# A graph layer on one core: both count steps of a round in one PSUM tile, copied by one ScalarE instruction

## The chip, the core and the metric

The kernel runs on one core of a Trainium2 chip. The metric is the device time of one execution in microseconds (us), the median of several runs. Times inside one execution come from the hardware profiler.

## The reference

The layer has 6250 nodes with 64 features and 206250 edges, sorted by their destination `dst`. What is computed:

```python
h = jnp.maximum(_layernorm(x, axis=-1), 0.0)
msg = node_feat[src] + edge_feat            # node_feat is h
agg = jax.ops.segment_sum(msg, dst, num_segments=node_feat.shape[0])
h = jax.nn.relu(agg @ W1 + b1)
return h @ W2 + b2                          # added to x
```

## The kernel before

Nodes are taken in 49 tiles of 128. Instead of gathering 206250 rows of `h`, the kernel builds, for a pair of node tiles, a matrix of counts: how often each source node occurs among the edges of each destination node. A source index is split into a low part of 7 bits and a high part below 49. For each destination node of the pair, VectorE makes one-hot rows of both parts for up to 64 edges (`hots`, L656: `lo_hot` with 128 columns and `hi_hot` with 50), and a matmul of 64 rows multiplies them (`count`, L810). That gives a 128x49 block of counts, in PSUM. ScalarE copies the blocks from PSUM to SBUF as bf16 (`copy_counts`, L387), turning their order round so that each of the 49 source tiles has its destination nodes side by side. Then TensorE multiplies `h`, held as three bf16 parts, by these counts: `high_sums` (L823, the two upper parts) and `low_sums` (L831, the lowest part), 49 matmuls of 256 columns each. `edge_sums` (L845) adds the edge features with one-hot windows `e_hot`. The result of a pair passes through two dense layers (`hidden`, L860, and `rows`, L867) and is stored.

The main loop runs over stages j, one for each pair of node tiles: 25 stages of counting (`DTS`), the last with a smaller tile alone, and one stage more to empty the pipeline. A full stage has 8 rounds v, and each round has two count steps, u = 2v and 2v + 1. A count step is 16 matmuls: 8 destination nodes of each of the two tiles. In stage j TensorE counts for pair j, sums for pair m = j - 1 with the counts made a stage earlier, and runs the dense layers of pair f = j - 2. In even rounds the sums are a quarter of `high_sums` (12 or 13 matmuls); in odd rounds a quarter of `low_sums` and half of an `edge_sums`. Round 0 has `hidden` as well, round 1 `rows`, round 3 ends with `turn_rel` (L795) and round 4 with `turn_codes` (L784, L785). In stage 0 there is nothing to sum, so only counting is done there.

Each engine runs its own program in written order, and semaphores join them. Those that matter here:

- `counted` goes up by one with the last matmul of each count step. `copy_counts` of the step waits for it, and so does `hots` before it overwrites a one-hot buffer of four steps.
- `copied` goes up by one with each copy. PSUM holds two count tiles of two banks each, `count_ps[0]` and `count_ps[1]`. A count step g writes `count_ps[g % 2]` and so waits until the copy of step g - 2 is done.

```python
if g >= 2:
    pe.wait_ge(copied, g - 1)
```

- `high_sums` of a stage waits once, in round 0, until all copies of the stage before are done.

Beside the copies, ScalarE does the following in each stage: `copy_agg` (L372) before the first copy, `relu` (L380) after the copy of step 1, `take_rel` (L363) after that of step 7 and `take_codes` (L354) after that of step 9. In stage 0 `take_part(1)` (L348), a copy of 3136 columns, stands after the copy of step 7.

GpSimd and the SyncE queue bring indices and edge rows; the change does not touch them.

## Time and profile before

| what | value |
|---|---|
| median of 3 runs | 562.6 us (560.68, 562.6, 565.33) |
| the profiled execution, its own time | 561.41 us |
| its span in the profile | 559.8 us |
| TensorE (PE) busy | 486.8 us, 87% of the span |
| VectorE (DVE) busy | 428.1 us, 76% |
| ScalarE (ACT) busy | 355.1 us, 63% |
| granted TensorE clock, mean over the span | 0.988 |

The span reaches from the first to the last instruction that was recorded, and the execution's own time is 1.6 us longer. PE stands for matmuls and PEld for the weight loads that run beside them. A name such as `L387` is a line of the kernel before. A group such as `counts<-count_ps` names the tile that is written and those that are read.

### The profile page before, as it was taken

How to read it: one execution, taken by the hardware profiler on the slowest of the kernel's cores; microseconds unless marked ns; L12 is line 12 of the kernel's file. 1: busy time of each engine (PE TensorE's matmuls, PEld its weight loads, DVE VectorE, ACT ScalarE, POOL GpSimd, SP SyncE). 2: the span in 40 equal slices, each digit the busy share in tenths (PEclk: the TensorE clock that was granted, in tenths of full speed). 3: DMA queues.
4: the chain of work that ended last, by engine and by line, in shares of the span. 5: the costliest groups of instructions: out<-in, count | busy, mean ns of one | idle time of the engine just before them, and what ended most of it. 6: DMA issues, size and time to landing. Idle time of an engine off the chain costs nothing.

```text
span 559.8 us, 27476 instructions
## 1 busy us (share of the span) xinstructions
PE 486.8 (87%) x12541; PEld 427.6 (76%) x12541; DVE 428.1 (76%) x456; ACT 355.1 (63%) x503; POOL 268.7 (48%) x249
## 2 busy tenths in 40 slices
PE   1014999999999999999999999999999999998996
PEld 1013788777888888888888888888888888887895
DVE  4999879667887797777787787777788779766941
ACT  3747667665766767656666666666676676575721
POOL 4483774484375366336357347417437535416200
PEclk9999999998999999989999999999999999899999
DMA  9575167453453543633634635435546354354300
GB/s 201 162 216 165 24 200 193 127 167 105 112 176 102 154 141 100 188 102 97 189 105 117 174 101 150 140 99 151 141 110 180 100 154 138 97 152 123 94 7 9
DMA packets 139623, 73.62 MB, mean 132 GB/s; under 512 B 23644, under 2 KB 137550, under 8 KB 139382
## 3 DMA queue, kind: packets, MB, share of 16 engines
q1 hardware_dynamic: 136105, 65.30, 42.4%
q0 software_dynamic: 3168, 4.90, 2.7%
q8 instruction: 99, 1.62, 1.2%
q10 hardware_dynamic: 234, 1.65, 0.9%
q14 instruction: 17, 0.14, 0.1%
HBM read 66.98 MB, written 4.86 MB: 128 GB/s over the span
## 4 chain that ended last, share of the span: by engine, by line
PE 84%; DVE 8%; issue 5%; ACT 1%; DMA 1%; another core or an unknown queue 0%; SPq 0%; DVEq 0%; ACTq 0%
PE sum_ps L823 25%; PE sum_ps L845 20%; PE count_ps L810 18%; PE sum_ps L831 14%; PE head_ps L860 3%; PE head_ps L867 3%; DVE lo_hot L656 2%; PE turn_ps L795 1%; DVE hi_hot L656 1%; DMA dst_sb<-in_dst 1%; DVE h_sb L555 1%; DVE mean L553 1%; DVE h_sb L568 1%; DVE var L561 1%; DVE h_parts L624 1%
## 5 line engine op out<-in xcount | busy, mean ns | idle before, releaser
L387 ACT CAST counts<-count_ps 128x784 bf16<-128x784 f32 x391 | 300.9, 817 | 129.0 <-PE count_ps L810 124.6
L656 DVE TENSOR_TENSOR lo_hot<-iota_lo,codes 128x4096 bf16<-128x4096 bf16 x98 | 224.1, 2286 | 66.8 <-PE count_ps L810 54.4
L823 PE MATMUL sum_ps<-counts,h_parts 128*128 128x256 bf16 (+1 forms) x1225 | 153.8, 277 | 0.0
L845 PE MATMUL sum_ps<-e_hot,edges 128*64 128x24 f32 x3528 | 129.6, 215 | 15.8 <-issue 15.6
L810 PE MATMUL count_ps<-hi_hot,lo_hot 64*128 64x49 bf16 x6256 | 124.9, 184 | 19.1 <-DVE hi_hot L656 11.5
L845 PEld LDWEIGHTS sum_ps<-e_hot,edges 128*64 128x64 f32 x3528 | 124.9, 138 | 20.5 <-issue 19.3
L810 PEld LDWEIGHTS count_ps<-hi_hot,lo_hot 64*128 64x128 bf16 x6256 | 101.5, 95 | 42.8 <-issue 13.4
L823 PEld LDWEIGHTS sum_ps<-counts,h_parts 128*128 128x128 bf16 x1225 | 114.1, 100 | 20.2 <-issue 0.2
L479 POOL TENSOR_SCALAR r_f<-rp_f 1x2 f32<-1x2 f32 x24 | 12.8, 533 | 188.9 <-DVE rp_f L630 188.8
L469 POOL DMA_INDIRECT g<-in_dst,row_i x49 | 88.0, 1796 | 18.3 <-issue 11.5
L656 DVE TENSOR_TENSOR hi_hot<-iota_hi,codes 128x1600 bf16<-128x1600 bf16 x98 | 96.5, 985 | 0.0
L831 PE MATMUL sum_ps<-counts,h_parts 128*64 128x256 bf16 (+1 forms) x1225 | 86.2, 275 | 0.0
L507 POOL TENSOR_SCALAR rel_rows<-dst_rows,tile_base 36x256 f32<-36x256 int32 (+1 forms) x25 | 71.6, 2864 | 4.4 <-DMA dst_rows<-in_dst 2.5
L496 POOL DMA_INDIRECT ell<-comb_rows,ell_idx x50 | 60.4, 1208 | 22.1 <-issue 17.0
L831 PEld LDWEIGHTS sum_ps<-counts,h_parts 128*64 128x64 bf16 x1225 | 59.7, 110 | 5.2 <-issue 0.2
L670 DVE TENSOR_TENSOR e_hot<-win_tab,rel_sb 128x864 f32<-128x864 f32 x49 | 54.8, 1118 | 6.1 <-ACT rel_sb L363 6.1
L372 ACT COPY agg_sb<-sum_ps 128x256 f32<-128x256 f32 (+1 forms) x25 | 9.2, 367 | 27.3 <-issue 11.9
L642 DVE SCALAR_TENSOR_TENSOR hi_m<-ell,node_f 128x64 bf16<-128x64 f32 x50 | 11.9, 278 | 17.4 <-DMA ell<-comb_rows,ell_idx 13.3
L784 PE MATMUL turn_ps<-ident_b,ell 128*128 128x128 bf16 x25 | 5.6, 223 | 21.4 <-DVE hi_m L642 19.0
L682 DVE TENSOR_TENSOR o_sb<-head_ps,x_sb 128x128 f32<-128x128 f32 (+1 forms) x25 | 7.1, 286 | 18.4 <-PE head_ps L867 18.4
L354 ACT COPY codes<-turn_ps 128x512 bf16<-128x512 bf16 x25 | 14.7, 587 | 9.9 <-PE turn_ps L785 9.9
L784 PEld LDWEIGHTS turn_ps<-ident_b,ell 128*128 128x128 bf16 x25 | 2.8, 112 | 21.9 <-issue 21.7
(108 smaller groups left out, 222.3 us busy)
## 6 DMA issues: line engine op xcount, KB each, us to landing
edges<-in_edge_attr SPq DMA_DIRECT2D x98, 576.0 KB
h_rows<-h_sb SPq DMA_DIRECT2D x1, 1568.0 KB, 10.1
x_sb<-in_x SPq DMA_DIRECT2D x4, 384.0 KB, 10.5
out<-o_sb SPq DMA_DIRECT2D x24, 64.0 KB, 3.7
comb_rows<-counts ACTq DMA_DIRECT2D x1, 1443.8 KB
dst_rows<-in_dst SPq DMA_DIRECT2D x49, 18.0 KB
ell<-comb_rows,ell_idx POOLq DMA_INDIRECT x50
g<-in_dst,row_i POOLq DMA_INDIRECT x49
```

Source lines behind the costliest of these rows:

```text
L387: nc.scalar.copy(counts[j % 2][:, :, 0:2 * half].rearrange("p s (h i) -> p h s i", h=2)[:, :, :, 8 * u:8 * u + 8], count_ps[g % 2][:, :, 0 ...
L469: nc.gpsimd.indirect_dma_start(out=g2[j % 2][:, h, :], out_offset=None, in_=dst.rearrange("(r e) -> r e", e=STEP), in_offset=bass.Indirect ...
L496: nc.gpsimd.indirect_dma_start(out=ell[j % 2][0:rows, h, :, :].rearrange("p s w -> p (s w)"), out_offset=None, in_=comb_dram[:, :], in_off ...
L507: nc.gpsimd.tensor_scalar(rel_rows[j % 2][0:n * CK, :], dst_rows[j % 2][0:n * CK, :], float(2 * j * P), tile_base[0:n * CK, 0:1], ALU.subt ...
L656: return nc.vector.tensor_tensor(out_ap.rearrange("p i (a t) -> p i a t", t=2), bc(table_ap.rearrange("p (o a t) -> p o a t", o=1, t=2), [ ...
L670: nc.vector.tensor_tensor(e_hot[h][:, :, :].rearrange("p (c k) w -> p c k w", k=KK), bc(win_tab[:, m // LAST, :, :].rearrange("p c (o w) - ...
L810: last = nc.tensor.matmul(count_ps[g % 2][:, h, i * NT:(i + 1) * NT], lo_hot[n % 2][rows, at, :], hi_hot[n % 2][rows, at, 0:NT], start=Tru ...
L823: nc.tensor.matmul(sum_ps[m % 2][:, 0:cols], parts[:, s, 0:2 * F], counts[m % 2][:, s, 0:cols], start=(s == 0), stop=False, skip_group_che ...
L831: last = nc.tensor.matmul(sum_ps[m % 2][half, 0:cols], parts[:, s, 2 * F:3 * F], counts[m % 2][:, s, 0:cols], start=False, stop=False, ski ...
L845: last = nc.tensor.matmul(sum_ps[m % 2][half, low:low + W], edges[t % SLOT_EDGES][:, c, k * F:(k + 1) * F], e_hot[h][:, i, :], start=False ...
L860: nc.tensor.matmul(hid_ps[:, 0:cols], w1_sb[:, :], agg_sb[:, 0:cols], start=True, stop=True).then_inc(hid_made, 1)
L867: last = nc.tensor.matmul(out_ps[0:n, h * F:(h + 1) * F], hid_sb[:, h * P:h * P + n], w2_sb[:, :], start=True, stop=True)
```

## The change

The four PSUM banks of the count steps become one tile, with the step of the round as an index of its own. ScalarE copies both steps of a round with one instruction of 1568 columns. The wait for `copied` now stands before the first step of a round alone, and it asks for the copy of the whole round before. The semaphore counts rounds. `relu` follows the copy of round 0, `take_rel` and `take_part(1)` that of round 3, and `take_codes` that of round 4, which are the places that they had. The last stage of counting has 7 steps, so its fourth round has a single step and a copy of 784 columns.

```diff
-        count_ps = [ps(f"count_ps{b}", [P, 2, 512]) for b in range(2)]
+        count_ps = ps("count_ps", [P, 2, 2, 512])
...
-                def copy_counts(j, u):
-                    g = step_index(j, u)
-                    act.wait_ge(counted, g + 1)
+                def copy_counts(j, v):
+                    n = min(2, steps_of(j) - 2 * v)
+                    act.wait_ge(counted, step_index(j, 2 * v) + n)
                     half = P if j < LAST else HALF
+                    first = 16 * v
                     nc.scalar.copy(
-                        counts[j % 2][:, :, 0:2 * half].rearrange("p s (h i) -> p h s i", h=2)[:, :, :, 8 * u:8 * u + 8],
-                        count_ps[g % 2][:, :, 0:8 * NT].rearrange("p h (i s) -> p h s i", s=NT)).then_inc(copied, 1)
+                        counts[j % 2][:, :, 0:2 * half].rearrange("p s (h i) -> p h s i", h=2)[
+                            :, :, :, first:first + 8 * n].rearrange("p h s (b i) -> p h s b i", b=n),
+                        count_ps[:, 0:n, :, 0:8 * NT].rearrange("p b h (i s) -> p h s b i", s=NT)).then_inc(copied, 1)
...
-                    for u in range(steps_of(j) if j < DTS else 0):
-                        copy_counts(j, u)
-                        if u == 1 and f >= 0:
+                    for v in range(rounds_of(j) if j < DTS else 0):
+                        copy_counts(j, v)
+                        if v == 0 and f >= 0:
                             relu(f)
-                        if j == 0 and u == 7:
+                        if j == 0 and v == 3:
                             take_part(1)
-                        if u == min(7, steps_of(j) - 1):
+                        if v == 3:
                             take_rel(j)
-                        if u == 9 and j + 1 < DTS:
+                        if v == 4 and j + 1 < DTS:
                             take_codes(j + 1)
...
-                    if g >= 2:
-                        pe.wait_ge(copied, g - 1)
+                    if u % 2 == 0 and g >= 2:
+                        pe.wait_ge(copied, round_index(j, u // 2))
                     for i in range(8):
...
-                            last = nc.tensor.matmul(count_ps[g % 2][:, h, i * NT:(i + 1) * NT],
+                            last = nc.tensor.matmul(count_ps[:, u % 2, h, i * NT:(i + 1) * NT],
...
-                                pe.wait_ge(copied, step_index(m, 0) + steps_of(m))
+                                pe.wait_ge(copied, round_index(m, rounds_of(m)))
```

The two new helpers are `rounds_of(j)`, which is half of `steps_of(j)` rounded up, and `round_index(j, v)`, which is 8j + v.

On TensorE, in rounds 2 and 3 of a full stage, stood before (the count matmuls are those of `count_ps`, and L845 is the end of an `edge_sums`):

```order
L810 MATMUL count_ps<-hi_hot,lo_hot 128x49 [waits copied,hots_made]
L810 MATMUL count_ps<-hi_hot,lo_hot 128x49 x15
L810 MATMUL count_ps<-hi_hot,lo_hot 128x49 [waits copied]
L810 MATMUL count_ps<-hi_hot,lo_hot 128x49 x15
L823 MATMUL sum_ps<-counts,h_parts 128x256 x12
L810 MATMUL count_ps<-hi_hot,lo_hot 128x49 [waits copied]
L810 MATMUL count_ps<-hi_hot,lo_hot 128x49 x15
L810 MATMUL count_ps<-hi_hot,lo_hot 128x49 [waits copied]
L810 MATMUL count_ps<-hi_hot,lo_hot 128x49 x15
L831 MATMUL sum_ps<-counts,h_parts 64x256 x12
L845 MATMUL sum_ps<-e_hot,edges 64x24 x18
```

At the same place stands now:

```order
L818 MATMUL count_ps<-hi_hot,lo_hot 128x49 [waits copied,hots_made]
L818 MATMUL count_ps<-hi_hot,lo_hot 128x49 x31
L831 MATMUL sum_ps<-counts,h_parts 128x256 x12
L818 MATMUL count_ps<-hi_hot,lo_hot 128x49 [waits copied]
L818 MATMUL count_ps<-hi_hot,lo_hot 128x49 x31
L839 MATMUL sum_ps<-counts,h_parts 64x256 x12
L853 MATMUL sum_ps<-e_hot,edges 64x24 x18
```

The matmuls stand in the same order. Of the two waits for `copied` in a round the first is left, and the copy that it asks for is now that of both steps of the round before.

On ScalarE, over a full stage from its round 5 to round 4 of the next, stood before:

```order
L387 CAST counts<-count_ps 128x2x49x8 x6
L372 COPY agg_sb<-sum_ps 128x256
L387 CAST counts<-count_ps 128x2x49x8 x2
L380 ACTIVATE hid_sb<-head_ps,b_col 128x256
L387 CAST counts<-count_ps 128x2x49x8 x6
L363 COPY rel_sb<-turn_ps 128x2x36
L387 CAST counts<-count_ps 128x2x49x8 x2
L354 COPY codes<-turn_ps 128x512
```

And now:

```order
L394 CAST counts<-count_ps 128x2x49x16 x3
L378 COPY agg_sb<-sum_ps 128x256
L394 CAST counts<-count_ps 128x2x49x16
L386 ACTIVATE hid_sb<-head_ps,b_col 128x256
L394 CAST counts<-count_ps 128x2x49x16 x3
L369 COPY rel_sb<-turn_ps 128x2x36
L394 CAST counts<-count_ps 128x2x49x16
L360 COPY codes<-turn_ps 128x512
```

Two copies of 784 columns have become one of 1568 everywhere, and the other work of ScalarE stands between the same rounds.

## Rows read from the trace of the kernel before

**Rows 1.** The page: busy time of the engines, its share of the span, instructions

```profile
PE 486.8 (87%) x12541; PEld 427.6 (76%) x12541; DVE 428.1 (76%) x456; ACT 355.1 (63%) x503; POOL 268.7 (48%) x249
```

**Rows 2.** The page: the chain that ended last, by engine

```profile
PE 84%; DVE 8%; issue 5%; ACT 1%; DMA 1%; another core or an unknown queue 0%; SPq 0%; DVEq 0%; ACTq 0%
```

**Rows 3.** Groups: busy, mean ns of one | idle before, what ended it

```profile
L387 ACT CAST counts<-count_ps 128x784 bf16<-128x784 f32 x391 | 300.9, 817 | 129.0 <-PE count_ps L810 124.6
L656 DVE TENSOR_TENSOR lo_hot<-iota_lo,codes 128x4096 bf16<-128x4096 bf16 x98 | 224.1, 2286 | 66.8 <-PE count_ps L810 54.4
```

**Rows 4.** Waits of TensorE for the copies: total us, times, longest us

```profile
PEld count_ps L810 <- ACT counts L387: 12.1, 35, 1.0
```

**Rows 5.** Timeline, round 2 of stage 13: start us, us taken, what, count

```profile
310.30 0.58 PE L810 MATMUL count_ps<-hi_hot,lo_hot 64*128 64x49 bf16 x32
310.71 1.53 ACT L387 CAST counts<-count_ps 128x784 bf16<-128x784 f32 x2 [0.97 <-PE count_ps L810]
310.81 1.48 PE L823 MATMUL sum_ps<-counts,h_parts 128*128 128x256 bf16 x12
...
312.23 0.58 PE L810 MATMUL count_ps<-hi_hot,lo_hot 64*128 64x49 bf16 x32
```

**Rows 6.** Timeline, from the end of round 3 to round 5 of stage 13

```profile
314.53 0.30 PE L795 MATMUL turn_ps<-wide,rel_rows 36*128 36x36 f32 x1
...
314.68 0.69 PE L810 MATMUL count_ps<-hi_hot,lo_hot 64*128 64x49 bf16 x30
...
315.21 1.53 ACT L387 CAST counts<-count_ps 128x784 bf16<-128x784 f32 x2
...
316.83 0.58 PE L810 MATMUL count_ps<-hi_hot,lo_hot 64*128 64x49 bf16 x32
```

**Rows 7.** Timeline, rounds 6 and 7 of stage 13

```profile
320.56 0.58 PE L810 MATMUL count_ps<-hi_hot,lo_hot 64*128 64x49 bf16 x32
...
320.98 1.53 ACT L387 CAST counts<-count_ps 128x784 bf16<-128x784 f32 x2 [1.49 <-PE count_ps L810]
...
322.60 0.58 PE L810 MATMUL count_ps<-hi_hot,lo_hot 64*128 64x49 bf16 x32
```

**Rows 8.** Groups by form: two longer copies of ScalarE

```profile
L354 ACT COPY codes<-turn_ps 128x512 bf16<-128x512 bf16 x25 | 14.7, 587 | 9.9 <-PE turn_ps L785 9.9
...
L345 ACT COPY h_parts<-h_sb 128x3136 bf16<-128x3136 bf16 x1 | 2.8, 2808 | 0.0
```

**Rows 9.** Timeline, stage 0 and the start of stage 1

```profile
37.57 2.96 ACT L387 CAST counts<-count_ps 128x784 bf16<-128x784 f32 x4 [1.28 <-PE count_ps L810]
...
38.43 0.38 PEld L810 LDWEIGHTS count_ps<-hi_hot,lo_hot 64*128 64x128 bf16 x16 [0.79 <-ACT counts L387]
...
43.65 0.84 PE L810 MATMUL count_ps<-hi_hot,lo_hot 64*128 64x49 bf16 x32 [3.98 <-DVE hi_hot L656]
...
47.40 2.81 ACT L348 COPY h_parts<-counts 128x3136 bf16<-128x3136 bf16 x1
...
50.22 1.55 ACT L387 CAST counts<-count_ps 128x784 bf16<-128x784 f32 x2
...
57.31 0.91 PE L810 MATMUL count_ps<-hi_hot,lo_hot 64*128 64x49 bf16 x32 [0.52 <-DVE hi_hot L656]
```

**Rows 10.** Timeline, rounds 2 and 3 of stage 2

```profile
82.52 0.58 PE L810 MATMUL count_ps<-hi_hot,lo_hot 64*128 64x49 bf16 x32
...
83.97 0.81 ACT L387 CAST counts<-count_ps 128x784 bf16<-128x784 f32 x1 [2.40 <-PE count_ps L810]
...
84.84 0.19 PEld L810 LDWEIGHTS count_ps<-hi_hot,lo_hot 64*128 64x128 bf16 x9 [0.60 <-ACT counts L387]
...
85.52 2.24 ACT L387 CAST counts<-count_ps 128x784 bf16<-128x784 f32 x3 [0.74 <-remote]
86.39 0.27 PEld L810 LDWEIGHTS count_ps<-hi_hot,lo_hot 64*128 64x128 bf16 x16 [0.81 <-ACT counts L387]
```

More of the change, by code:

```diff
@@ L45, in steps_of, with rounds_of, round_index @@
         return 16 if j < LAST else HALF // 8
+    def rounds_of(j):
+        return -(-steps_of(j) // 2)
+    def round_index(j, v):
+        return 8 * j + v
     def step_index(j, u):
```

## The prediction

> **What bounds the kernel now.** I read the page's busy times first, then the chain that ended last, the groups, the waits, and last the timeline of single rounds.
>
> TensorE is busy for 486.8 of 559.8 us, VectorE for 76% and ScalarE for 63% [rows 1]. The chain that ended last is TensorE for 84% of the span and ScalarE for 1% [rows 2]. So what TensorE loses in a stage comes out at the end, and what ScalarE saves is worth nothing by itself. ScalarE's 391 count copies are its largest group, 817 ns each, and before them it sat idle for 129.0 us, of which 124.6 us were ended by the count matmuls: it waits for TensorE [rows 3]. VectorE too sits idle for 66.8 us before its one-hots, mostly for TensorE [rows 3]. TensorE's count steps wait for the copies for only 12.1 us in all, in 35 places [rows 4].
>
> The timeline of a middle stage gives the numbers that decide. In round 2 of stage 13 the 32 count matmuls start at 310.30 and end at 310.88. The two copies run from 310.71 to 312.24, side by side with 12 sums, and the counts of round 3 start at 312.23 [rows 5]. The first of these copies starts before the second count step is done, and its half of PSUM is free long before 312.23. So TensorE goes from counts to sums to counts without a stop, while the second copy ends just as the next round's counts begin. That is the point: the two half tiles let the copy begin early and the counts begin before the copies are all done. The change takes both away.
>
> **What the change removes.** ScalarE issues 195 fewer instructions. Two copies back to back take 1.53 us [rows 5]. The long one costs the 817 ns of one copy plus 784 further columns [rows 3]. The price of a column comes from ScalarE's two other long copies: (2808 - 587) / (3136 - 512) = 0.846 ns [rows 8]. So one copy of 1568 columns is 817 + 784 x 0.846 = 1480 ns. The saving is 0.05 us a round on an engine that is not the bound, and I cost it at nothing. The same holds for the second wait of each round, which is gone: no engine works there.
>
> The long copy itself is not in the trace, so I bound it. From below: columns alone and no fixed cost, 1568 x 0.846 = 1.33 us. From above: twice the single copy, 1.63 us [rows 3]. I take 1.48 us, since both rows of the slope are copies of the same engine and 784 lies between them. The deeper source pattern could add something that no row shows, and the upper end allows for it.
>
> The Trainium skill (ScalarE: Activation LUTs, section What ACT_TABLE_LOAD costs) gives 186 ns plus 0.833 ns a column for an instruction without pointer operands, which would be 1.49 us here by an estimate from that page. For 784 columns it gives 839 ns against the 817 measured here. The sum would grow by 0.01 us in each waiting round, some 0.6 us in all.
>
> **What it adds: a wait in the even rounds.** The copy now starts after the second step. A copy starts about 0.04 us after the matmul that releases it: the first step of round 2 ends 0.21 us before the second, at 310.67 by the same timeline, and its copy starts at 310.71 [rows 5]. TensorE takes up its work 0.05 us after a copy ends, where it really waits for one: in stage 0 the first copy starts at 37.57 and takes 0.82, to 38.39, and the count step that waits for it starts at 38.43 [rows 9]. I round to 0.05. So from the end of a round's counts to the next possible counts it is 0.04 + 1.48 + 0.05 = 1.57 us.
>
> - Round 2 to 3: counts end at 310.88, so the next can start at 312.45. They started at 312.23 [rows 5]. Wait 0.22 us.
> - Round 4 to 5: counts end at 315.37 and the next started at 316.83 [rows 6]. The next can start at 316.94. Wait 0.11 us.
> - Round 6 to 7: counts end at 321.14, next at 322.60, now 322.71 [rows 7]. Wait 0.11 us.
> - Round 0 has `hidden` in it as well, and odd rounds have the longer sums. Round 3: counts end at 312.81, plus 1.57 is 314.38, and TensorE reaches the next counts at 314.53 or later [rows 5, 6]. No wait, with 0.15 us to spare, and the others have more.
>
> That is 0.44 us in a full stage. Going through all rounds of the timeline in this way, round 2 is so in 21 stages, round 4 in 23 and round 6 in 18; the rest have other stops there already. 21 x 0.22 + 23 x 0.11 + 18 x 0.11 = 9.1 us. Behind the waiting count step stand the sums, the turns and the dense layers of TensorE, in written order, so nothing fills the gap. VectorE waits for `counted` and ScalarE too, so they move along. Both have slack.
>
> **Stage 0.** Here nothing is summed, and the round is counts, then copy, in series. 32 counts take 0.84 us here against 0.58 later [rows 5, 9]. In series a round takes 0.84 + 1.57 = 2.41 us. From round 2, which starts at 43.65 for want of one-hots [rows 9]: its copy ends at 46.0, that of round 3 at 48.45. Then come `take_part(1)`, 2.81 us, and `take_rel`, to 51.4. The copy of round 4 ends at 52.9 (before: two copies from 50.22 to 51.77 [rows 9]). Round 5 counts from 52.95, round 6 from 55.4, round 7 from 57.8, and round 0 of stage 1 from 60.2 instead of 57.31 [rows 9]. Before, VectorE's one-hots were the limit at 57.31 [rows 9]; they will be ready when the copy now comes. That is 2.9 us, of which I take 2.7, as the sums behind it also had a short stop of their own.
>
> **Stages 2 and 3.** Here the releases come late. In stage 2 the counts of round 2 end at 83.10 and the first copy starts only at 83.97; the next at 85.52 [rows 10]. The round's copy would then start at 85.52 and end at 87.0, and round 3's counts, which stretched from 84.84 to 86.77, would run from 87.05 to 87.65. That is 0.8 us more, and stage 3 looks alike: 1.6 us.
>
> **The sum.** 9.1 + 2.7 + 1.6 = 13.4 us. On the profiled execution's own 561.4 us that makes 574.8. Its time is 1.2 us under the median of the runs, 562.6, so I say 575 us. The ends of the copy's price: at 1.33 us only round 2 of each stage would wait, 0.07 us, and stage 0 would lose 1.6 us, so with the late releases about 4.5 us in all, 566 us. At 1.63 us every wait grows by 0.15: 62 x 0.15 = 9.3 us, plus 1 us in stage 0, and 585 us.
>
> A rule of the Trainium skill (Perfetto Trace Analysis, section Matmuls) speaks against the change: independent matmul groups should rotate through PSUM banks so that the evacuation of one overlaps the next group's matmuls. Rows 5 show that overlap, the copy at 310.71 beside the second step. By that rule the kernel gets slower, which is my forecast, while the sum above says by how much.
>
> **Rivals.**
>
> *The waits are swallowed (chance 0.12).* TensorE has other stops in a stage; the chain has 5% of "issue" [rows 2], a good part of it in the edge sums of round 5. If these stops were tied to a time and not to TensorE's place, the 0.33 us lost in rounds 2 and 4 would be won back there. Against it: the stops come at the same place of each stage. What is left is round 6 and stages 0 to 3: 2.0 + 2.7 + 1.6 = 6.3 us, so 568 us, or 566 with a cheap copy. That is within 1%.
>
> *Late releases become exposed (chance 0.15).* In stage 2 a semaphore reaches ScalarE 0.9 us late or more [rows 10]. Before, two tiles hid most of that. If it strikes one more round in each stage, in rounds 3 or 7 with their small slack, at some 0.3 us, that is 7 us more: 582 us.
>
> *It is faster (chance 0.04).* The second wait of each round stands in the middle of the count stream, in 195 rounds. If such a wait costs TensorE's sequencer time, its removal gives that back; and where TensorE waits for the copies today, at most 12.1 us [rows 4], ScalarE's shorter work could help too. This wins only if it brings more than 13.4 / 196 = 0.07 us a round. With 0.1 us a round it would be 561.4 + 13.4 - 19.6 = 555 us. Against it: 32 count matmuls with the wait in their midst take 0.58 us [rows 5], which is 18 ns a matmul and the last one's full length included, so there is hardly 0.1 us to find; and the waits of today lie largely in stage 0, where the sum shows a loss.
>
> *It does not do what it says.* The order of instructions shows one copy a round and one wait, so I give no chance to this.
>
> **How the numbers follow.** Forecast 0.69, swallowed 0.12, exposed 0.15, faster 0.04. A measurement of this kernel can tell about 1%, 5.6 us, from no change. The forecast's own spread leaves little below 568.2: slower 0.87, within 1% 0.10, faster 0.03. The range is 567 to 583: it takes in the swallowed waits and most of the exposed case, and leaves out the far ends of the copy's price.
>
> **What would show it right or wrong.** In the changed kernel's groups the copy should be x195 of 1568 columns at 1.48 us, with ScalarE's busy time about 10 us less. The waits of TensorE's counts for ScalarE should appear in rounds 3, 5 and 7 of each stage, some 60 of them beside those of stage 0, with the counts of round 3 starting 1.57 us after the counts of round 2 end. Stage 1 should begin near 60.2 us. A full stage should take 20.5 us instead of 20.1. If the copy takes 1.35 us or less, or if stages last 20.1 us in spite of the waits, I am wrong.

## The result and the profile after

| | before | changed |
|---|---|---|
| median of the runs | 562.3 us | 612.7 us (606.9 to 615.3) |
| the profiled execution, own time and span | 561.4, 559.8 us | 612.4, 610.8 us |
| granted TensorE clock, mean | 0.988 | 0.959 |

The ratio is 1.088, with a 95% interval from 1.079 to 1.097: 8.8% slower, where 575 us, 2.2% slower, was forecast. The direction is right and the size is far off, above the range. Here and below a time is the median of all executions of a kernel, and a ratio leaves out those slow ones that come out over 1.5% above the fastest of the same kernel.

The page of the changed kernel: busy time, the chain that ended last by engine, and the groups that answer to [rows 1 to 3].

```profile
PE 507.7 (83%) x12541; PEld 436.9 (72%) x12541; DVE 431.3 (71%) x456; ACT 345.7 (57%) x308; POOL 245.1 (40%) x249
...
PE 65%; ACT 17%; another core or an unknown queue 9%; DMA 3%; issue 2%; DVE 2%; POOL 0%; SPq 0%; ACTq 0%; DVEq 0%
...
L394 ACT CAST counts<-count_ps 128x1568 bf16<-128x1568 f32 x196 | 286.5, 1462 | 203.0 <-PE count_ps L818 145.3
L664 DVE TENSOR_TENSOR lo_hot<-iota_lo,codes 128x4096 bf16<-128x4096 bf16 x98 | 224.7, 2293 | 125.0 <-remote 86.2
```

The copy is as forecast: 1462 ns on average, where 1480 was worked out. ScalarE is busy 9.4 us less [rows 1] and now stands on the chain for 17% of the span (1% in [rows 2]). The new thing is in VectorE's row. Its one-hots waited 66.8 us before [rows 3] and wait 125.0 now, of which 86.2 are put down to "remote": the profile saw the semaphore come and no instruction that ended then. ScalarE's copies have the same. From the waits of the changed kernel (engine, line, whom for: total, times, longest):

```profile
DVE lo_hot L664 <- remote: 86.2, 22, 4.2
ACT counts L394 <- remote: 56.6, 22, 4.1
...
PE count_ps L818 <- ACT counts L394: 28.6, 30, 2.3
```

Twenty-two times is once in almost every stage. The timeline of stage 13 shows the place. Its first four lines are rounds 2 and 3, the rest is round 5 and what follows.

```profile
340.19 0.75 PE L818 MATMUL count_ps<-hi_hot,lo_hot 64*128 64x49 bf16 x32
...
340.98 1.47 ACT L394 CAST counts<-count_ps 128x1568 bf16<-128x1568 f32 x1 [1.59 <-PE count_ps L818]
...
342.50 0.48 PEld L818 LDWEIGHTS count_ps<-hi_hot,lo_hot 64*128 64x128 bf16 x32 [0.42 <-ACT counts L394]
342.50 0.58 PE L818 MATMUL count_ps<-hi_hot,lo_hot 64*128 64x49 bf16 x32
...
347.21 0.58 PE L818 MATMUL count_ps<-hi_hot,lo_hot 64*128 64x49 bf16 x32
347.61 1.00 POOL L504 DMA_INDIRECT ell<-comb_rows,ell_idx  x1 [0.47 <-issue]
...
348.92 0.95 POOL L504 DMA_INDIRECT ell<-comb_rows,ell_idx  x1 [0.30 <-issue]
...
349.70 0.34 PE L853 MATMUL sum_ps<-e_hot,edges 128*64 128x24 f32 x5 [0.41 <-issue]
...
350.45 1.47 ACT L394 CAST counts<-count_ps 128x1568 bf16<-128x1568 f32 x1 [2.66 <-remote]
...
350.52 2.29 DVE L664 TENSOR_TENSOR lo_hot<-iota_lo,codes 128x4096 bf16<-128x4096 bf16 x1 [4.07 <-remote]
```

Rounds 2 and 3 are as forecast. The copy starts 0.04 us after the counts end at 340.94, lasts 1.47, and the next counts start at 342.50, 1.56 us after that end (forecast 1.57). In round 5 the counts end at 347.79 by the matmul rows, but the copy starts only at 350.45, and VectorE's next one-hots wait for the same count step and start at 350.52. Both see the step some 2.7 us late. (The ends of matmuls are modelled by the profile; the trace also has the time at which the semaphore `counted` went up, and it went up 2.64 us after that end, 0.02 us before the copy started.) Just then GpSimd runs the two indirect DMAs that fetch edge slots (L504, `gather_slots`; "slot DMAs" from here on). And TensorE's own edge matmuls stop in between, for which the row at 349.70 stands.

What comes behind, in the same kernel and engines:

```profile
352.06 0.58 PE L818 MATMUL count_ps<-hi_hot,lo_hot 64*128 64x49 bf16 x32 [0.92 <-ACT counts L394]
...
352.58 2.67 PE L831 MATMUL sum_ps<-counts,h_parts 128*128 128x256 bf16 x13
```

The counts of round 6 wait 0.92 us for that late copy, and 13 sums take 2.67 us, where 13 took 1.59 in the first profile. The stretches of the changed kernel show the clock (PE busy, PEld, DVE, ACT, POOL, then the granted clock, the DMA share and GB/s):

```profile
347.00:352.00 5.00, 3.11 (x83) 2.57 (x80) 1.48 (x1) 2.20 (x3) 4.06 (x6) 1.00 0.82 245
352.00:355.30 3.30, 3.24 (x51) 2.29 (x53) 2.94 (x3) 1.47 (x1) 2.84 (x3) 0.64 0.02 5
```

After the stops of round 5 the granted clock averages 0.64 in this stretch: it falls from full speed (2.4 GHz) to half (1.2 GHz) for 3.4 us. There are 14 such drops before the end of the kernel, 13 of them behind a late round 5, and the profile of before had four.

The kernel before had this lateness too, in a milder form, in rows that were not read for the forecast. These are rounds 5 and 6 of its stage 13, from the timeline:

```profile
316.83 0.58 PE L810 MATMUL count_ps<-hi_hot,lo_hot 64*128 64x49 bf16 x32
...
317.33 1.00 POOL L496 DMA_INDIRECT ell<-comb_rows,ell_idx  x1 [0.48 <-issue]
...
317.42 0.82 ACT L387 CAST counts<-count_ps 128x784 bf16<-128x784 f32 x1
...
318.64 0.94 POOL L496 DMA_INDIRECT ell<-comb_rows,ell_idx  x1 [0.30 <-issue]
318.68 0.81 ACT L387 CAST counts<-count_ps 128x784 bf16<-128x784 f32 x1 [0.44 <-PE count_ps L810]
```

The second count step ends at 317.41 and its copy starts at 318.68, 1.27 us later. Round 5 lasted 3.7 us there against 2.3 where nothing is late, and it takes 4.8 us in the changed kernel. By stage, from the starts of the counts in the timelines, means over stages 1 to 23:

| round | 0 | 1 | 2 | 3 | 4 | 5 | 6 | 7 | stage |
|---|---|---|---|---|---|---|---|---|---|
| before, us | 2.59 | 2.87 | 2.12 | 2.50 | 2.26 | 3.42 | 2.20 | 2.55 | 20.5 |
| changed, us | 2.61 | 2.90 | 2.24 | 2.31 | 2.42 | 4.47 | 2.85 | 2.72 | 22.5 |

A round is counted here from its first weight load to that of the next. 2.0 us a stage over 23 stages is some 47 us, and stage 0 grew by 3.8 us, from 20.4 to 24.2. Of the 47 us, round 5 has 24, round 6 15 and round 7 4; the rest is about 3 us.

### The profile page after: what moved, and what is told of

It reads as the page before. It is cut to its first block, busy times and chain, and to the rows that moved or that the text cites. A ratio compares the mean times of both kernels' runs of the same rounds, so it can differ in the third digit from the quotient of the medians.

```text
span 610.8 us, 27281 instructions
## 1 busy us (share of the span) xinstructions
PE 507.7 (83%) x12541; PEld 436.9 (72%) x12541; DVE 431.3 (71%) x456; ACT 345.7 (57%) x308; POOL 245.1 (40%) x249
## 4 chain that ended last, share of the span: by engine, by line
PE 65%; ACT 17%; another core or an unknown queue 9%; DMA 3%; issue 2%; DVE 2%; POOL 0%; SPq 0%; ACTq 0%; DVEq 0%
PE sum_ps L831 20%; PE count_ps L818 17%; ACT counts L394 13%; PE sum_ps L853 12%; PE sum_ps L839 10%; PE head_ps L868 3%; PE head_ps L875 2%; ACT codes L360 2%; DMA lo_hot<-in_src 2%; DMA comb_rows<-counts 1%; PE turn_ps L803 1%; ACT counts L331 1%; ACT counts L333 1%; DMA ell<-comb_rows,ell_idx 1%
## 5 line engine op out<-in xcount | busy, mean ns | idle before, releaser
L394 ACT CAST counts<-count_ps 128x1568 bf16<-128x1568 f32 x196 | 286.5, 1462 | 203.0 <-PE count_ps L818 145.3
L664 DVE TENSOR_TENSOR lo_hot<-iota_lo,codes 128x4096 bf16<-128x4096 bf16 x98 | 224.7, 2293 | 125.0 <-remote 86.2
L831 PE MATMUL sum_ps<-counts,h_parts 128*128 128x256 bf16 (+1 forms) x1225 | 166.3, 292 | 0.6 <-issue 0.6
L831 PEld LDWEIGHTS sum_ps<-counts,h_parts 128*128 128x128 bf16 x1225 | 119.7, 104 | 26.4 <-issue 1.1
L487 POOL TENSOR_SCALAR r_f<-rp_f 1x2 f32<-1x2 f32 x24 | 5.2, 216 | 258.3 <-DVE rp_f L638 258.2
L664 DVE TENSOR_TENSOR hi_hot<-iota_hi,codes 128x1600 bf16<-128x1600 bf16 x98 | 100.8, 1028 | 0.0
L477 POOL DMA_INDIRECT g<-in_dst,row_i x49 | 79.2, 1616 | 18.3 <-issue 11.5
L504 POOL DMA_INDIRECT ell<-comb_rows,ell_idx x50 | 55.4, 1107 | 23.2 <-issue 17.9
L839 PEld LDWEIGHTS sum_ps<-counts,h_parts 128*64 128x64 bf16 x1225 | 60.2, 111 | 5.5 <-issue 0.2
L515 POOL TENSOR_SCALAR rel_rows<-dst_rows,tile_base 36x256 f32<-36x256 int32 (+1 forms) x25 | 49.8, 1994 | 5.6 <-DMA dst_rows<-in_dst 3.7
L523 POOL TENSOR_TENSOR x_sb<-x_sb,b_all 128x128 f32<-128x128 f32 (+1 forms) x25 | 35.5, 1422 | 1.6
L868 PE MATMUL head_ps<-agg_sb,w_sb 128*128 128x256 f32 (+1 forms) x50 | 17.8, 438 | 0.7 <-ACT agg_sb L378 0.5
```

The source lines that it names most:

```text
L394: nc.scalar.copy(counts[j % 2][:, :, 0:2 * half].rearrange("p s (h i) -> p h s i", h=2)[:, :, :, first:first + 8 * n].rearrange("p h s (b ...
L477: nc.gpsimd.indirect_dma_start(out=g2[j % 2][:, h, :], out_offset=None, in_=dst.rearrange("(r e) -> r e", e=STEP), in_offset=bass.Indirect ...
L504: nc.gpsimd.indirect_dma_start(out=ell[j % 2][0:rows, h, :, :].rearrange("p s w -> p (s w)"), out_offset=None, in_=comb_dram[:, :], in_off ...
L515: nc.gpsimd.tensor_scalar(rel_rows[j % 2][0:n * CK, :], dst_rows[j % 2][0:n * CK, :], float(2 * j * P), tile_base[0:n * CK, 0:1], ALU.subt ...
L523: nc.gpsimd.tensor_tensor(x_sb[:, tiles, :], x_sb[:, tiles, :], bc(b2_all[:, :].rearrange("p (o f) -> p o f", o=1), [P, tiles_in(f), F]), ...
L664: return nc.vector.tensor_tensor(out_ap.rearrange("p i (a t) -> p i a t", t=2), bc(table_ap.rearrange("p (o a t) -> p o a t", o=1, t=2), [ ...
```

## The experiments

### Each half of the change alone

The change does two things at once: the copy starts only after both steps, and the next round waits for all of it. Two kernels do one each, with the two tiles and the two copies of before.

```diff
 # e1_whole_wait
-                    if g >= 2:
-                        pe.wait_ge(copied, g - 1)
+                    if u % 2 == 0 and g >= 2:
+                        pe.wait_ge(copied, g)
 # e2_late_copies
-                    act.wait_ge(counted, g + 1)
+                    act.wait_ge(counted, step_index(j, min(u | 1, steps_of(j) - 1)) + 1)
```

> The kernel before, with its two tiles and two copies, but the first count step of a round now waits for both copies of the round before. Theory 'both together': the loss comes only when the copy starts late and the counts wait for all of it. Then this half alone costs little: the second copy ends 1.53 + 0.41 us after the round's first count, so round 3 begins 0.06 us later and no other, 1 to 3 us in all, 563 to 566 us. Rival 'the whole wait alone': if the late release of round 5 hits any kernel whose round 6 waits for the whole of round 5, most of the 50 us is here already, 590 us or more.

> The kernel before, but both copies of a round start only after its second count step, as the one long copy does; each count step still waits for its own tile alone. Theory 'both together': the first tile is free 0.04 + 0.82 us after the counts, the second 1.57 us after them, and the second step needs it 0.2 us later than the first; no wait in full stages, some 1 to 4 us from stage 0, 563 to 567 us. Rival 'the late start alone': 590 us or more, with round 6 at half clock as in the changed kernel.

Measured: e1 531.75 us, ratio 0.997 (0.994 to 1.000); e2 533.42 us, ratio 1.002 (0.999 to 1.005). Each half costs nothing that counts here. But the kernel before took 532.9 us beside them and not 562. That was the surprise of this first set of experiments (a set is what ran together on one chip), and it took over the study. Neither half was ever measured where the kernel before takes 562 us, so what each costs there is not shown.

### Without the slot DMAs

In these two the indirect DMAs of `gather_slots` are issued in stages 0 and 1 alone, and what waited for their landing waits for their indices instead. Part of the computation is left out by it.

```diff
-                    for h in range(2):
+                    for h in range(2 if j < 2 else 0):
...
-                    dve.wait_ge(ell_in[j % 2], 32 * (j // 2 + 1))
+                    if j < 2:
+                        dve.wait_ge(ell_in[j % 2], 32)
+                    else:
+                        dve.wait_ge(idx_made, j + 1 + (j == LAST))
```

> The changed kernel without the indirect DMAs that bring the slots of edges (ell) in stages 2 to 24; the slots of stages 0 and 1 are used again, so that part of the computation is left out. Theory 'slot gathers': these DMAs, issued at the start of round 5, hold up the end of the count step that runs beside them. Then round 5 shrinks from 4.8 us to 2.4, the copy of round 5 starts 0.04 us after the counts, the drops of the clock in round 6 go, a stage takes 20.1 less 1.4 plus 0.45 us = 19.2, and the kernel 545 to 555 us. Rival 'edge traffic': the loads of edge rows, which fill the DMA engines in the same 5 us, do it, and nothing changes: 605 to 615 us.

> The kernel before with the same indirect DMAs left out. Theory 'slot gathers': round 5 shrinks from 3.7 us to 2.3, a stage takes 18.8 us and the kernel 530 to 538 us, so that the two kernels without these DMAs differ by the 10 to 15 us of the forecast. Rival 'edge traffic': no change, 560 to 565 us.

Measured: e3 540.09 us, ratio to before 1.014 (1.008 to 1.020); e4 529.99 us, 0.993 (0.988 to 0.998). By their numbers both seem to bear out the theory (e3 lies even below its 545 us), but the kernel before, with all its slot DMAs, was at 532.9 us in the same set. So these runs had no lateness of 1 us and more to remove, and their times say nothing on its cause. What they say: the DMAs cost at most 1% or so where nothing is late. Their traces show a little more, which is told below.

### The changed kernel where round 5 is on time

> The changed kernel itself again, with its profile, since the kernel before took 532.9 us where the last four ran and 562 us where the change was measured. If the 30 us between these two times of the kernel before are the late end of round 5, the changed kernel has no late round 5 here either and costs what the forecast's mechanism gives: the waits of rounds 2, 4 and 6 (9 us) and stage 0 (3 us), 542 to 548 us, 2 to 3% slower. Rival: the change brings the late round 5 by itself; then it is 9% slower here too, 575 us or more.

> The kernel before, unchanged, for its profile on the same chip. If round 5 ends in time here, a full stage takes 18.8 us (20.1 in the first profile) and the copies of round 5 start 0.7 us apart (1.26 in the first profile); 530 to 535 us. If this chip is like the first, 562 us.

Measured: r5 541.78 us against 532.19, ratio 1.016 (1.008 to 1.024). The kernel before, run once more with its profile (r6), gave 532.37 us. So the change costs 9.6 us here and 50 us in the first set. This is round 5 of the kernel before in this set (r6_before), from its timeline:

```profile
302.25 0.58 PE L810 MATMUL count_ps<-hi_hot,lo_hot 64*128 64x49 bf16 x32
302.75 1.01 POOL L496 DMA_INDIRECT ell<-comb_rows,ell_idx  x1 [0.47 <-issue]
302.83 1.53 ACT L387 CAST counts<-count_ps 128x784 bf16<-128x784 f32 x2
...
304.06 2.12 POOL L496 DMA_INDIRECT ell<-comb_rows,ell_idx  x1 [0.30 <-issue]
304.55 0.58 PE L810 MATMUL count_ps<-hi_hot,lo_hot 64*128 64x49 bf16 x32
```

And this is r5_after, the changed kernel:

```profile
305.29 0.58 PE L818 MATMUL count_ps<-hi_hot,lo_hot 64*128 64x49 bf16 x32
305.69 1.01 POOL L504 DMA_INDIRECT ell<-comb_rows,ell_idx  x1 [0.47 <-issue]
306.01 1.47 ACT L394 CAST counts<-count_ps 128x1568 bf16<-128x1568 f32 x1
...
307.01 2.19 POOL L504 DMA_INDIRECT ell<-comb_rows,ell_idx  x1 [0.31 <-issue]
307.62 0.58 PE L818 MATMUL count_ps<-hi_hot,lo_hot 64*128 64x49 bf16 x32
```

The same DMAs start at the same point of the round, and nothing is late: the two copies follow each other in 1.53 us in the first, and in the second the copy starts 0.14 us after the counts end at 305.87. Round 5 takes 2.3 us in both. One row differs between the two kinds of sets: in the middle stages the second slot DMA occupies GpSimd for 2.1 to 2.2 us here, and for 0.95 us where round 5 is late. The 0.14 us are not nothing either. This is the same round of e3, where no slot DMA runs:

```profile
307.19 0.58 PE L821 MATMUL count_ps<-hi_hot,lo_hot 64*128 64x49 bf16 x32
...
307.81 1.47 ACT L394 CAST counts<-count_ps 128x1568 bf16<-128x1568 f32 x1
```

The copy starts 0.04 us after the counts end at 307.77, in this and in every other stage. In r5_after it is 0.14 us in the stages that have the slot DMAs at this place and 0.04 us in stages 22 and 23, which do not. So even in a set on time the slot DMAs hold the semaphore back, by 0.1 us, and it is on time when they are taken away.

Round by round, median before to changed: round 2 from 1.95 to 2.15 us, round 4 from 2.29 to 2.39, round 6 from 2.04 to 2.17, the others unchanged. That is 0.43 us a stage (forecast 0.44). By the mean the stages differ less, 19.45 against 19.21 us, 5.4 us in all: before has more other stops in this pair of traces, one drop of the clock in stage 2 among them. Stage 1 begins at 60.09 us (forecast 60.2; in the changed kernel's first profile 61.38). In the waits of r5_after:

```profile
PEld count_ps L818 <- ACT counts L394: 27.7, 72, 1.8
```

Seventy-two waits for the copy, with those of stage 0 in them (forecast some 60 beside stage 0); before there were 35 [rows 4].

### The slot DMAs held back

The changed kernel, with one wait more on GpSimd:

```diff
+                    if j >= 2:
+                        pool.wait_ge(counted, step_index(j - 2, 12))
                     for h in range(2):
```

> The changed kernel, but GpSimd issues the indirect DMAs for the slots of edges of stage j + 2 only when round 5 of stage j has been counted, some 0.5 to 3 us later. Where round 5 is late in the changed kernel, theory 'slot gathers' has it on time now and the kernel 20 to 40 us faster than the changed one, or the lateness moves into round 6; where it is not late, no difference to the changed kernel within 3 us.

Measured 541.11 us, ratio 1.012 (1.001 to 1.023), in the set of r5_after. That is the changed kernel's time, as it should be where nothing is late. In its trace the copy of round 5 starts 0.04 us after the counts in every stage, where it was 0.14 in r5_after: moving the slot DMAs away does what leaving them out did.

### Both halves with two copies

Both edits of e1 and e2 together, and nothing else.

> The kernel before with both edits of the first two runs at once: both copies of a round start after its second count step, and the next round waits for both. That is the change with two instructions of 784 columns where it has one of 1568. Theory 'both together': the pair of copies takes 1.53 us where the long one takes 1.46, so it must be slower than before by as much as the change or a little more, 10 to 15 us (2 to 3%), on a chip where round 5 ends in time. On a chip where it ends late, as in the first profiles: 50 us or more. Rival 'the long instruction itself costs': then this kernel stays within 3 us of the kernel before.

Measured 620.75 us against 561.4, ratio 1.105 (1.100 to 1.110). This set was of the late kind. The kernel has two copies of 784 columns and loses no less than the change, which cost 8.8% in another late set. So the long instruction is not the cost; the tie between copy and counts is. Its trace shows the same lateness: in its stage 12, the counts of round 5 end at 329.09, the two slot DMAs start at 328.85 and 330.16, and the first copy starts at 331.71, 2.6 us late. The clock dropped 16 times before the end.

```profile
328.51 0.58 PE L810 MATMUL count_ps<-hi_hot,lo_hot 64*128 64x49 bf16 x32
328.85 1.01 POOL L496 DMA_INDIRECT ell<-comb_rows,ell_idx  x1 [0.47 <-issue]
...
330.16 0.94 POOL L496 DMA_INDIRECT ell<-comb_rows,ell_idx  x1 [0.30 <-issue]
...
331.71 1.53 ACT L387 CAST counts<-count_ps 128x784 bf16<-128x784 f32 x2 [2.68 <-remote]
```

### Looking for a late set again

The next kernels were those of above once more, in the hope of a late set. None came.

> Again the changed kernel without the slot DMAs of stages 2 to 24 (part of the computation is left out), in the hope of a chip on which the kernel before takes 562 us. Theory 'slot gathers': they are what ends round 5 late on such a chip; then round 5 takes 2.3 us, the clock stays up, and the kernel takes 538 to 550 us. Rival 'edge traffic' or anything else in the round: 600 us or more. On a chip of the other kind: 540 us as before, and nothing is told.

> Again the kernel before with the wait for the whole round alone. On a chip with the late round 5: its second count step ends 1.2 us late in the kernel before, and the copy of it is done at 0.8 us after that, while the next counts come 1.9 us after it, so a wait for it costs nothing: 560 to 568 us. If the whole wait is what draws the lateness out to 2.6 us: 585 us or more. On a chip of the other kind: 532 us.

> Again the kernel before with the late start of the copies alone. On a chip with the late round 5: the first copy of round 5 starts 1.2 us later than before, and the counts of round 6 still need only that one at first: 562 to 575 us. If the late start is what draws the lateness out to 2.6 us and lowers the clock: 585 us or more. On a chip of the other kind: 533 us.

> Again the changed kernel with the slot DMAs held back until round 5 has been counted. On a chip with the late round 5, theory 'slot gathers': the counts of round 5 end in time, and the lateness, if it follows the DMAs, falls on the edge sums of rounds 5 and 6: 560 to 600 us, and less than the changed kernel by 10 us or more. Rival: no difference to it, 605 to 615 us. On a chip of the other kind: 541 us.

> The changed kernel without the slot DMAs of stages 2 to 24 (part of the computation is left out), once more, since three of the five chips so far end round 5 in time. On a chip where the kernel before takes 562 us, theory 'slot gathers': 538 to 550 us. Rival: 600 us or more. On a chip of the other kind 540 us.

> The kernel before with the late start of both copies alone, once more. On a chip where the kernel before takes 562 us: 562 to 575 us if the lateness of round 5 grows only when both halves of the change are there, 590 us or more if the late start alone draws it out. On a chip of the other kind 533 us.

> The changed kernel without the slot DMAs of stages 2 to 24 (part of the computation is left out). On a chip where the kernel before takes 562 us, theory 'slot gathers': 538 to 550 us. Rival: 600 us or more. On a chip of the other kind 540 us again.

> The changed kernel without the slot DMAs of stages 2 to 24 (part of the computation is left out). On a chip where the kernel before takes 562 us, theory 'slot gathers': 538 to 550 us. Rival: 600 us or more. On a chip of the other kind 540 us again.

| run | us | beside the kernel before at |
|---|---|---|
| s1_after_no_slots | 541.54, ratio 1.019 (1.006 to 1.031) | 531.58 |
| s2_whole_wait | two executions, 530.5 and 545.8 | 531.58 |
| s3_late_copies | two executions, 531.2 and 543.6 | 531.58 |
| s4_after_gather_later | 540.47, ratio 1.017 (1.009 to 1.024) | 531.58 |
| t1_after_no_slots | 538.93, ratio 1.010 (1.006 to 1.014) | 534.05 |
| t2_late_copies | two executions, 540.9 and 555.0 | 534.05 |
| u1_after_no_slots | 538.31, ratio 1.011 (0.999 to 1.022) | 533.13 |
| u2_after_no_slots | 539.25, ratio 1.013 (1.010 to 1.016) | 532.36 |

All sets here were on time, so these runs do not tell the causes apart. They fit the on-time cost: the changed kernel and its variants stand 1.0 to 1.9% above the kernel before in all of them, with intervals up to 1% wide on either side. For the halves, s2, s3 and t2, a single execution each is left to compare, 530.5, 531.2 and 540.9 us, which settles nothing. The expectations spoke of two kinds of chip, and that fell as well. The chip of s and u1 was on time there and late when v1 and v2 ran on it, and the chip of r8 was late then and on time for u2. So the lateness is no property of a chip alone.

### A step held by hand

To see what a late step costs each kernel, the second count step of round 5 is made to wait, in stages 0 to 21, for a small memset that GpSimd runs between its two slot DMAs.

```diff
                         ).then_inc(ell_in[j % 2], 16)
+                        if j >= 2 and h == 0:
+                            nc.gpsimd.memset(mark[:, :], 0.0).then_inc(slots_asked, 1)
...
+                    if u == 11 and j + 2 < LAST:
+                        pe.wait_ge(slots_asked, j + 1)
                     for i in range(8):
```

> The kernel before, with the late count step made by hand on any chip: in stages 0 to 21 TensorE waits, before the second count step of round 5, until GpSimd has run the first of the two slot DMAs of that round (a small memset behind it tells so). That holds the step by some 1.2 us, as round 5 had it in the first profile of the kernel before. A stage should take 20.1 us instead of 18.8 and the kernel 558 to 564 us. If the clock drops often after such a stop it is more, up to 580 us.

> The changed kernel with the same hold. Theory 'the same lateness costs the changed kernel more' (its long copy of round 5 is then waited for and the clock drops in round 6): 590 to 612 us. Rival 'the lateness itself has to grow, as it did from 1.2 to 2.6 us': with 1.2 us in both, the changed kernel stands the usual 8 to 11 us above the held kernel before, 567 to 575 us.

This set was late by itself: before 561.72 us. Measured: v1 567.78 us, ratio 1.011 (1.003 to 1.019); v2 598.91 us, 1.067 (1.049 to 1.084). v2 falls in the 590 to 612 us of its first theory, and is 31 us above v1 where the rival had 8 to 11. But the test is not the one that was meant, because the lateness by hand and the other one came together; and the drop of the clock in round 6, part of that theory, is absent from v2's profile. The traces tell more than the times. Round 5 of stage 13 in v2:

```profile
339.82 0.38 PE L824 MATMUL count_ps<-hi_hot,lo_hot 64*128 64x49 bf16 x16
340.22 1.00 POOL L506 DMA_INDIRECT ell<-comb_rows,ell_idx  x1 [0.47 <-issue]
341.21 0.09 POOL L512 MEMSET mark<- 1x1 f32 x1
341.36 0.38 PE L824 MATMUL count_ps<-hi_hot,lo_hot 64*128 64x49 bf16 x16 [1.16 <-POOL mark L512]
341.53 0.94 POOL L506 DMA_INDIRECT ell<-comb_rows,ell_idx  x1 [0.23 <-issue]
...
343.00 1.47 ACT L396 CAST counts<-count_ps 128x1568 bf16<-128x1568 f32 x1 [2.60 <-PE count_ps L824]
```

The hold moved the second step behind the first slot DMA. It ends at 341.74, and its copy starts 1.26 us later, at 343.00. In the changed kernel it was 2.66 us. It looks as if half the lateness had gone with one of the DMAs, but the times against the first slot DMA say something else. Lined up (late sets; on-time sets for comparison; all in us, and from the start of the round's first slot DMA where it says so):

| kernel | step's end, from the first DMA's start | copy starts late by | copy's start, from the first DMA's start |
|---|---|---|---|
| before, stages 5 to 21 | 0.08 | 1.24 to 1.27 | 1.3 |
| before, stage 4 | 0.20 | 2.56 | 2.8 |
| before, stages 1 to 3 and 22 | the DMAs come some 5 us later or more | not late | |
| changed | 0.18 | 2.66 (1.97 in four of the stages) | 2.8 (2.1) |
| changed, stage 2 | 0.84 | 2.12 | 3.0 |
| r8, both halves | 0.24 | 2.6 | 2.9 |
| v1, held past the first DMA | 1.61 | 0.4 to 0.5 (1.1 in four of the stages) | 2.1 (2.7) |
| v2, held past the first DMA | 1.52 | 1.26 (0.5 in two of the stages) | 2.8 (2.1) |
| before, on time | 0.08 | not late | |
| changed, on time | 0.18 | 0.14 | |

The last column is the one that repeats. However early or late the step ends, its semaphore comes 1.3, or 2.0 to 2.1, or 2.7 to 3.0 us after the first slot DMA starts: in the five traces of late sets all 104 late round 5 steps do so, though their ends lie from 0.08 to 1.8 us behind that start. So the moment of release goes with the DMAs and not with the step. v2's step is less late because it ends 1.3 us later and is released at the same moment. That also says what 0.1 us decide: a step that ends 0.08 us after the first DMA's start was released at 1.3 us, just as the second DMA starts, and one that ends at 0.18 us or later never was; it came with the next moment or the one behind. Why these are the moments is not shown.

The second thing in v2 is the clock. In the profiled execution its mean is 0.996, with one drop before the end where the changed kernel had 14. Its round 5 is as long as there (4.76 us in the middle, against 4.83), and its rounds 6 are back at 2.17 us. The span is 593.7 us instead of 610.8. Most of the 17 us between these are what the clock drops took; by stages of the changed kernel with the same 2.66 us of lateness, one without a drop lasts 21.6 us and one with a drop mostly 23.2 to 23.5, so a drop costs some 1.6 us. Why the clock held in v2, with stops as long, is not shown, and it did not always hold: v2's other execution took 602.5 us at a mean clock of 0.979.

### A look inside the first profile

Two traces speak against the other suspect, the loads of edge rows, which share the same 5 us. In the profile of before, in stage 1, the slot DMAs start only at 76.15, and the round 5 of that stage runs from 70.27. Its stretch beside that of stage 5, which is late (same columns as above):

```profile
70.20:72.60 2.40, 2.40 (x85) 2.26 (x84) 2.40 (x4) 2.02 (x3) 0.56 (x1) 1.00 1.05 311
153.60:157.40 3.80, 2.98 (x86) 2.64 (x86) 1.86 (x1) 2.11 (x3) 2.94 (x4) 1.00 1.03 308
```

The DMA engines moved 311 GB/s in the first and 308 in the second. The first round was on time and TensorE never stopped; the second was 1.4 us longer. Round 5 of stage 22 of the changed kernel, which has no slot DMAs beside it, shows 346 GB/s from 552 to 554.5 us and no lateness either. So the traffic of the edge loads alone does not do it. In the profile of before, the late stages are 4 to 21, and these are the ones with slot DMAs beside the step. In the changed kernel they are 1 to 21, with the same rule.

The slot DMAs are not the only ones. GpSimd also issues indirect DMAs that fetch rows of `dst` (`g`, L469 in the kernel before), and the late copies of stage 2 that the forecast had read [rows 10] stand beside two of these:

```profile
82.63 1.04 POOL L469 DMA_INDIRECT g<-in_dst,row_i  x1 [0.17 <-issue]
...
83.98 0.96 POOL L469 DMA_INDIRECT g<-in_dst,row_i  x1 [0.30 <-issue]
```

The copy of the first step starts at 83.97 and that of the second at 85.52, which is 1.34 and 2.89 us after 82.63: the same moments again. Over all 391 count steps in each of the five late traces, 258 semaphores came more than 0.3 us behind the last matmul. Each of the 258 steps has an indirect DMA of GpSimd running at its end, or starting at most 1.5 us before or 0.9 us after it. Of the steps that have none, no semaphore was more than 0.08 us late. The reverse does not hold: more than half of the steps with such a DMA beside them were on time.

One stage of before, stage 4, happens to have the changed kernel's timing. Its round 5, from the timeline of the kernel before:

```profile
133.29 0.58 PE L810 MATMUL count_ps<-hi_hot,lo_hot 64*128 64x49 bf16 x32
133.68 1.01 POOL L496 DMA_INDIRECT ell<-comb_rows,ell_idx  x1 [0.47 <-issue]
134.24 0.81 ACT L387 CAST counts<-count_ps 128x784 bf16<-128x784 f32 x1 [0.26 <-PE count_ps L810]
134.99 0.94 POOL L496 DMA_INDIRECT ell<-comb_rows,ell_idx  x1 [0.30 <-issue]
136.44 0.81 ACT L387 CAST counts<-count_ps 128x784 bf16<-128x784 f32 x1 [1.39 <-remote]
...
137.11 0.58 PE L810 MATMUL count_ps<-hi_hot,lo_hot 64*128 64x49 bf16 x32
```

The second step ends at 133.88, 0.20 us after the first slot DMA starts, and its copy starts 2.56 us late. So the jump from 1.27 to 2.6 us belongs to where the step ends against the first slot DMA, and needs no change of the kernel. In the changed kernel the wait between rounds 4 and 5 puts it there in every stage: 0.1 us of waiting doubles the lateness. And the same stage shows what two tiles were worth. Round 6 begins at 137.11, while the late copy is still running, since it needs only the first one, of 134.24. Round 5 lasts 3.82 us there, hardly more than the 3.7 of its neighbours, and 4.84 in the changed kernel with the same lateness.

## Why the prediction was right or wrong

**The direction was right, and so was the mechanism of the waits, in the sets on time.** There each half is free, e1 and e2, and only the tie of both costs. The copy was 1462 ns (forecast 1480), counts to counts 1.56 us (1.57), the waits 0.43 us a stage (0.44), stage 1 at 60.09 us (60.2). On time, the change costs 9.6 us in the medians, 8.4 us in the spans of r5_after and r6_before. In those spans 5.4 us are stages 1 to 23 and 2.8 us stage 0, where the forecast had 9.1 and 2.7 us; its 1.6 us for late releases in stages 2 and 3 did not show there. (Its 13.4 us on top of the median, 562.6, would be 576 us and not 575, which changes nothing.) But the time that was forecast is that of a late set, and there the right direction says little: four fifths of the loss came by a way that the sum has at nothing.

**The step that failed is the sentence "No wait, with 0.15 us to spare, and the others have more", which puts round 5 at nothing.** It priced every round with a copy that starts 0.04 us after the counts. That number came from round 2 [rows 5] and was used for round 5 unread. The timeline of before had the exception in every middle stage: the second copy of round 5 started 1.27 us late. With two tiles that was hidden, since the next counts needed only the first copy at first. What it cost there was TensorE's own stops in the edge matmuls, 0.4 us at a time. The forecast read round 4 and round 6 on either side of it [rows 6, 7] and left the 3.7 us between 316.83 and 320.56 to "other stops", as a good part of the 5% of "issue".

**The rival "late releases become exposed" was the true one, and its term was mis-sized.** It was given a chance of 0.15 and 0.3 us a stage, in rounds 3 or 7. Round 5 grew by 1.05 us a stage and round 6 by 0.65, because three things came together. The lateness itself grew, from 1.27 to 2.66 us, as the wait before round 5 shifted the step by 0.1 us against the slot DMAs. The long copy, which the next counts now need whole, was waited for, 0.92 us in stage 13. And the clock, which the forecast took as given, dropped 14 times instead of four.

**The account of the 51 us between the two spans.** About 8 us are the waits and stage 0, as the on-time set gives them. The 14 drops of the clock took some 22 us at 1.6 us each; in the kernel before a stage with a drop lasted 1.5 to 3.3 us longer than its neighbours, some 9 us for its four, so some 13 to 14 us are the clock. That is an estimate from the lengths of stages. The remaining 29 or so are the longer stop in round 5 and the wait for its copy.

**What stays open.** That the indirect DMAs of GpSimd are what holds the semaphore is borne out by three things: no step without one beside it is late, the release comes at fixed times after their start even when the step is moved by hand, and in the sets on time the 0.1 us that they hold it go when they are left out or moved (e3, r7). It is not shown by leaving them out in a late set, since no such run met one. How they hold it is open, and so is what makes a set late or on time. Nor does any late set tell whether the late copies or the whole wait alone would have cost much there.

## What to carry to other kernels

Joining two small PSUM evacuations into one saves only a fixed cost of ScalarE, and takes from TensorE the right to go on while they run. Before doing it, look from the end of the counts to the next write of that tile: here 1.35 us of sums stood against 1.57 us of copy, and only 0.1 to 0.2 us were missing, in three rounds of eight. And check each round of the stage for its own release time; two buffers hid a late semaphore here which one buffer turned into a stop, and behind 13 of 21 such stops TensorE came back at half clock. Where one kernel has two times that differ by 5% from set to set, look for what differs in its own trace before comparing it with another kernel.

## What the runs showed of the hardware

- The same kernel before took 532 us in six sets of runs and 562 in three, as medians. The difference is the 1.4 us of round 5 in 18 stages, and for the rest three more drops of the clock; it did not stay with a chip.
- In the late sets the semaphore of a count step that ended beside two indirect DMAs of GpSimd went up 0.4 to 2.7 us after its last matmul, at 1.3, 2.0 to 2.1 or 2.7 to 3.0 us after the first of them started, while TensorE ran on with its next matmuls. In the on-time sets it was 0.12 to 0.15 us beside the same DMAs and 0.02 us without. In the profiles of before and of the changed kernel TensorE's edge matmuls, for which the profile shows nothing to wait for, stopped for 0.4 us at a time in the same stretch.
- The granted clock fell for 3.4 us at a time to half speed: four times in the profile of before, 14 times in the changed kernel, 16 in r8, once in v2, whose round 5 was as long but had its stop elsewhere in it. A drop made a stage of the changed kernel some 1.6 us longer.
